# Handing out the QKV tail and the next layernorm between the heads of an attention core: a macaron block (FFN, sliding-window attention, FFN) on eight cores

## What is computed

```python
x = x + 0.5 * ffn(layernorm(x), W_r, W_k, W_v, mu_r, mu_k)
x = x + attn(layernorm(x), Wqkv, bqkv, Wo, bo, rope_cache)
x = x + 0.5 * ffn(layernorm(x), W_r, W_k, W_v, mu_r, mu_k)

def ffn(x, ...):                       # x_prev: x shifted by one row
    xr = mu_r * x + (1 - mu_r) * x_prev
    xk = mu_k * x + (1 - mu_k) * x_prev
    return sigmoid(xr @ W_r.T) * (relu(xk @ W_k.T) ** 2 @ W_v.T)

def attn(h, ...):                      # 16 heads of 64, window of 128 rows to both sides
    q, k, v = split(h @ Wqkv + bqkv)
    q, k = rope(q), rope(k)
    probs = softmax(q @ k.T / 8 + mask)
    return (probs @ v) @ Wo + bo
```

## Time and profile before

| what | before |
|---|---|
| median of 2 runs | 1699.78 us (1692.81 to 1706.74) |
| profiled execution | 1695.23 us |
| its span, slowest core | 1693.7 us |
| spans of the eight cores | 1675.3 to 1693.7 us |
| TensorE busy | 983.9 us, 58% |
| VectorE busy | 613.5 us, 36% |
| ScalarE busy | 496.7 us, 29% |

### The profile page before, as it was taken

How to read it: one execution, slowest core, us unless ns; L and a number is a source line. 1 busy time by engine, 2 the same in 40 slices (tenths; PEclk the granted TensorE clock), 3 DMA queues, 4 the chain that set the end, 5 groups by cost and what they waited for, 6 DMA issues and landing times.

```text
span 1693.7 us, 18587 instructions; the slowest of 8 cores (1675.3 to 1693.7 us)
## 1 busy us (share of the span) xinstructions
PE 983.9 (58%) x4645; PEld 416.1 (25%) x4645; DVE 613.5 (36%) x1674; ACT 496.7 (29%) x1054; POOL 38.4 (2%) x71
## 2 busy tenths in 40 slices
PE   0077614767436556636666666677666353677666
PEld 0033202223112222212222222233222121233222
DVE  1164404544312223341333444433233324444552
ACT  0233402233112332222332333333332123334231
POOL 1000000000100000000000000000000010000000
PEclk9998866888768667766777766776777565888878
DMA  9924593232651112693222222212222534233222
GB/s 165 180 55 105 104 119 97 75 93 69 207 141 31 32 38 63 95 113 68 63 63 63 63 63 53 42 39 50 45 50 50 150 103 114 69 106 94 68 69 69
DMA packets 224372, 141.15 MB, mean 83 GB/s; under 512 B 195472, under 2 KB 197648, under 8 KB 224080
## 3 DMA queue, kind: packets, MB, share of 16 engines
q0 software_dynamic: 16592, 50.08, 15.2%
q1 hardware_dynamic: 193088, 48.25, 15.0%
q10 hardware_dynamic: 14592, 41.63, 7.2%
HBM read 86.47 MB, written 39.85 MB: 75 GB/s over the span
## 4 chain that ended last, share of the span: by engine, by line
PE 36%; DVE 21%; DMA 17%; issue 9%; ACT 7%; SPq 7%; ACTq 2%; DVEq 1%; POOL 0%; POOLq 0%
PE pb L601 15%; SPq L137 7%; DMA ln_fm_s<-ln_tm 6%; PE pb L401 6%; PE pb L708 5%; DMA ln2fm_s<-ln_tm 5%; PE pb L735 4%; DVE xkm_s L346 3%; PE pb L369 3%; DVE xrm_s L341 3%; DMA kfm_s<-kpre_s 3%; DVE attn_tm_s L766 2%; PE pb L606 2%; ACT qsq L207 2%; ACT probsT_s L717 2%
## 5 line engine op out<-in xcount | busy, mean ns | idle before, releaser
L601 PE MATMUL pb<-warena,ln2fm_s 128*128 128x512 f16 x912 | 254.8, 430 | 299.3 <-DMA ln2fm_s<-ln_tm 299.3
L401 PE MATMUL pb<-warena,kfm_s 128*128 128x512 f16 x560 | 158.1, 446 | 163.7 <-DMA kfm_s<-kpre_s 163.7
L722 DVE TENSOR_TENSOR probsT_s<-probsT_s,gates_sb 128x256 bf16<-128x256 bf16 x272 | 79.4, 292 | 460.4 <-ACT probsT_s L717 421.3
L369 PE MATMUL pb<-warena,xrm_s 128*128 128x512 f16 x560 | 140.1, 408 | 127.7 <-DVE stats L211 53.1
L601 PEld LDWEIGHTS pb<-warena,ln2fm_s 128*128 128x128 f16 x912 | 87.8, 106 | 433.5 <-issue 370.7
L717 ACT ACTIVATE probsT_s<-pb 128x384 bf16<-128x384 f32 x272 | 131.7, 491 | 70.1 <-PE pb L708 61.7
L708 PE MATMUL pb<-qpl_s,kpl_s 65*128 65x128 f16 x816 | 115.9, 274 | 52.5 <-DMA kpl_s<-kaug_s 32.5
L369 PE MATMUL pb<-warena,xkm_s 128*128 128x512 f16 x560 | 126.6, 379 | 0.0
L401 PEld LDWEIGHTS pb<-warena,kfm_s 128*128 128x128 f16 x560 | 61.1, 111 | 257.9 <-issue 213.9
L379 ACT ACTIVATE r_sb_s<-pb 128x512 f16<-128x512 f32 x70 | 38.9, 595 | 274.2 <-DVE xr_sb L414 138.0
L204 ACT ACTIVATE ln_tm<-xr_sb 128x1024 f16<-128x1024 f32 x56 | 58.9, 1052 | 187.2 <-issue 63.6
(11 more groups left out here) (82 smaller groups left out, 808.9 us busy)
## 6 DMA issues: line engine op xcount, KB each, us to landing
xr_sb<-xscr POOLq DMA_DIRECT2D x36, 512.0 KB, 4.1
xr_sb<-x ACTq DMA_DIRECT2D x20, 512.0 KB, 4.6
xscr<-xr_sb ACTq DMA_DIRECT2D x19, 512.0 KB, 2.9
xscr<-xr_sb POOLq DMA_DIRECT2D x17, 512.0 KB, 3.4
out<-xr_sb ACTq DMA_DIRECT2D x16, 512.0 KB, 2.7
wqkv<-wqkv POOLq DMA_DIRECT2D x1, 6144.0 KB, 59.3
warena<-wqkv ACTq DMA_DIRECT2D x3, 2048.0 KB, 28.8
warena<-ffn ACTq DMA_DIRECT2D x3, 2048.0 KB, 20.6
```

What stands on the lines that cost most here:

```text
L369: t.matmul(pb[bk][:, :], xm[:, gp, c, 128 * ti:128 * (ti + 1)], warena[:, c, woff + 512 * js:woff + 512 * (js + 1)], start=(c == 0), stop= ...
L401: P.op("t", lambda t, bk=bk, c=c, pp=pp, js=js: t.matmul(pb[bk][:, :], kfm[:, pp, c, :], warena[:, c, 2 * DM + 512 * js:2 * DM + 512 * (js ...
L601: P.op("t", lambda t, bk=bk, c=c, par=par, js=js: t.matmul(pb[bk][:, :], ln2fm[:, par, c, :], warena[:, c, 512 * js:512 * (js + 1)], start ...
L722: P.op("v", lambda v, hp=hp, gi=gi: v.tensor_tensor(AP(probsT, hp * 384, [[4 * 384, 128], [256, 2], [1, 128]]), AP(probsT, hp * 384, [[4 * ...
```

## The change

`emit_qkv_tail` becomes a generator: it has a `yield` at eight places and stops there. A second generator, `emit_ln2_steps(j)`, holds the same instructions as `emit_ln2(j)` with five `yield`s between its pieces, the last piece being the transpose. The loop makes one feeder of the two, tail of j and then layernorm of j+1, and `emit_attn_core` takes the next piece from it at the end of each of its 18 steps. What is left is emitted behind the core; iterations without a core run the feeder in one go. No instruction is added, removed or resized. The diff, with the repeated body of the layernorm cut:

```diff
--- before.py
+++ after.py
@@ -645,6 +645,7 @@
                     .rearrange("p (h d) -> p h d", h=NH), ALU.mult),
                     waits=[("s", evw)] + ([("v", v_cq)] if which == "q" else []),
                     fence=(which == "k"), incs=[("v", 1)])
+                yield
                 P.op("v", lambda v, sv=sv, par2=par2, SS=SS: v.tensor_tensor(
                     t2[:, :].rearrange("p (h b d) -> p h b d", h=NH, b=2), sv,
                     SS[:, par2, :].rearrange("p (h b d) -> p h b d", h=NH, b=2), ALU.mult),
@@ -687,9 +693,48 @@
                  waits=[("v", rope_tok["k"])] + kpl_free[j % 4], incs=[(sn, 16)])
             tr_tok[j] = (sn, P.n(sn))
 
-        def emit_attn_core(i):
+        def emit_ln2_steps(j):
+            par = j % 2
+            sl = lambda c: stats[:, par, c:c + 1]
+            P.op("a", lambda a: a.activation(ln_tm[:, par, :], xr_sb[:, j % 8, :], AF.Copy,
+                                             accum_out=sl(0)),
+                 waits=[xtok[j]] + lnT_free[par] + stats_free.pop(par, []),
+                 incs=[("s", 1)])
+            P.op("a", lambda a: a.activation(qsq[:, :], xr_sb[:, j % 8, :], AF.Square,
+                                             accum_out=sl(1)),
+                 waits=list(qsq_free[0]) + qsq_waw[:], incs=[("s", 1)])
+            qsq_waw[:] = [("s", P.n("s"))]
+            s_sq = P.n("s")
+            yield
...
+            wtok = P.n("v")
+            yield
+            stok = emit_rstd([par], wtok)
+            yield
+            lt = emit_ln_apply(xr_sb[:, j % 8, :], par, par, stok)
+            ln2_tok[j] = lt
+            yield
+            sn = f"yl{par}"
+            P.op("y", YT(ln2fm[:, par, :, :], ln_tm[:, par, :]),
+                 waits=[("v", lt)] + ln2fm_free[par] +
+                       ([(sn, P.n(sn))] if P.n(sn) > 0 else []),
+                 incs=[(sn, 16)])
+            lnT_free[par] = [(sn, P.n(sn))]
+            y_ln2[j] = (sn, P.n(sn))
+
+        def emit_attn_core(i, feeder=None):
             par = i % 2
             win = [(i - 1) % 4, i % 4, (i + 1) % 4]
+            feed = (lambda: next(feeder, None)) if feeder is not None else (lambda: None)
             gi = 1 if i == 3 else (2 if i == 18 else 0)
             LAG = 2
             for hh in range(NH + LAG):
@@ -751,6 +796,7 @@
                             attn_un[:, h * 65:(h + 1) * 65], pb[bk][:, 0:65]),
                             waits=[("t", pv_tok[(i, h)])] + wv, incs=[("v", 1)])
                         bank_free[bk_pv] = [("v", P.n("v"))]
+                feed()
             t_last = pv_tok[(i, NH - 1)]
             for sl in win:
                 kpl_free[sl] = [("t", sc_tok[(i, NH - 1)])]
@@ -818,11 +864,16 @@
         emit_ln2(1)
         for j in range(1, NT):
             emit_qkv(j)
+
+            def mk_feeder(j=j):
+                yield from emit_qkv_tail(j)
+                if j + 1 < NT:
+                    yield from emit_ln2_steps(j + 1)
+            fd = mk_feeder()
             if QT0 <= j - 2 <= QT1:
-                emit_attn_core(j - 2)
-            emit_qkv_tail(j)
-            if j + 1 < NT:
-                emit_ln2(j + 1)
+                emit_attn_core(j - 2, feeder=fd)
+            for _ in fd:
+                pass
             if j == 1 or j == 19:
                 slot_free[j % 8] = ("v", ln2_tok[j])
             if QT0 <= j - 3 <= QT1:
```

More of the change, by code:

```diff
@@ L688, in emit_qkv_tail @@
             tr_tok[j] = (sn, P.n(sn))
-        def emit_attn_core(i):
+        def emit_ln2_steps(j):
[11 more added lines that the diff above has]
+            yield
+            P.op("v", lambda v: v.tensor_scalar(sl(2), sl(0), 1.0 / DM, None, ALU.mult),
+                 waits=[("s", s_sq)], incs=[("v", 1)])
+            P.op("v", lambda v: v.tensor_tensor(sl(3), sl(2), sl(2), ALU.mult), fence=True,
+                 incs=[("v", 1)])
+            yield
+            P.op("v", lambda v: v.scalar_tensor_tensor(sl(4), sl(1), 1.0 / DM, sl(3),
+                                                       ALU.mult, ALU.subtract),
+                 fence=True, incs=[("v", 1)])
+            P.op("v", lambda v: v.tensor_scalar(sl(4), sl(4), 1e-5, None, ALU.add),
+                 fence=True, incs=[("v", 1)])
+            wtok = P.n("v")
[4 more added lines that the diff above has]
+            ln2_tok[j] = lt
+            yield
+            sn = f"yl{par}"
[6 more added lines that the diff above has]
+        def emit_attn_core(i, feeder=None):
             par = i % 2
             win = [(i - 1) % 4, i % 4, (i + 1) % 4]
+            feed = (lambda: next(feeder, None)) if feeder is not None else (lambda: None)
             gi = 1 if i == 3 else (2 if i == 18 else 0)
```

## The result

The changed kernel takes 1539.47 us (median of 11 runs, 1531.97 to 1568.57) against 1701.37 us of the kernel before (10 runs): ratio 0.9061, 95% interval 0.9027 to 0.9094. Ratios here compare fast runs alone: in some runs of any of these kernels the cores of one die show a lower granted clock and the time is some per cent longer, as in the run of 1568.57. The forecast was 1565 in a range of 1505 to 1630, so direction and range held, and the gain was undersized by some 26 us. The profiled execution's slowest core has a span of 1538.5 us (before: 1693.7).

The account below looks back on a forecast made before the run. TensorE's 299.3 us wait for the layernorm's transpose, queued behind the core, was taken as the bound. Savings of 111+3+20 = 134 us off 1695.2 gave 1561, plus 4.6 for the timed runs: 1565, range 1505 to 1630.

Parts of the forecast that it names:

- the sum: Whole kernel: 111 us from 14 regular iterations, 3 from iteration 7, 20 from the stage's end, 134 us saved.
- the two timed runs: Kernel before: median 1699.8 us, 4.6 above the profiled execution, so the forecast went from 1561 to 1565.
- TensorE waits for `ln2fm` because of the queues, and the wait goes: Ahead of QKV: 299.3 us idle for layernorm's transpose, queued behind a core it doesn't need; regular iterations no longer wait.
- The core by hand, 20.0 us: Attention core, followed instruction by instruction with the fed steps: grows from 12.65 to 20.0 us, +7.35.
- The walk: Attention core's hand-followed timeline: Square from 5.2, reduce and max end at 9.4, layernorm's square 13.6, last PV about 20.0.
- Wo 6.3 and QKV 12.9: Behind the core: output projection stays 6.3 us; QKV falls from 15.0 to 12.9 at 2.4 GHz; period 39.2.
- The transpose comes in time, with some 4 us to spare: Behind the core: layernorm's transpose issued at 18.35, there by 22.1 to 22.5, while wo lasts until 26.3.
- Iteration 7 at 70: Iteration beside the weight casts: 70 us instead of 72.7, 3 us saved, as transposes starting earlier still mostly wait.
- The stage's end, 20 us: End of attention stage: 32.5 us wait goes, wo(17) waits for its transpose behind weight loads; 76.5 becomes 56.1 us.
- a period of 58: Iteration 7: the figure if transposes advance beside the casts from their earlier start; the sum would be 12 us lower.
- The ScalarE floor: Rival for the core: delays hide behind one another, core 16.3 us, period 35.5, total 1511; chance 0.17.
- The collapse of the lag: Rival for the core: two-head lag fails, each head 2.1 us, core 34, period 53.2, total about 1785; chance 0.03.

Follow-up runs that it names:

- the two runs with one part fed: Changed kernel with only the QKV tail fed into the core: 1578.04 us, ratio 0.931; with only the layernorm fed: 1711.64 us, ratio 1.0072.
- split step: Changed kernel with one more `yield`, between the layernorm's copy and its square: 1536.85 us, ratio 0.907.
- early rope: Changed kernel with the first four fed steps (rope of q and k) emitted ahead of the core: 1530.3 us, ratio 0.8993.
- ScalarE lighter: Changed kernel with the layernorm's copy and square reading 64 of 1024 columns, so another output: 1519.54 us, ratio 0.8957.

## Why the prediction held, point by point

The mechanism held but for the wait at the stage's end, and the sizes erred mostly to one side. In the attention stage 164 us were saved where the sum had 134: 20 of the difference are the 14 regular iterations, 11 the stage's end, and iteration 7 takes back 1. Outside the stage 9 us were lost that the forecast put at nothing (the start and the second FFN stage), so the total came out nearer to the forecast than the stage did. That part is luck. The last 4.6 us of the gap are those that the forecast added for the two timed runs: after the change the profiled execution, 1540.04 us, is no faster than the median.

- *TensorE waits for `ln2fm` because of the queues, and the wait goes.* Right. It is gone from the regular iterations, and the two runs with one part fed show that both chains had to move. I had named only the layernorm's transpose as what gates QKV; that the copies into `qaug` wait for k's transpose was not in the prediction, and it decides as soon as the tail is late.
- *The core by hand, 20.0 us.* It is 18.8 to 19.1. The growth was mis-sized by 1.2 us of 7.35. The walk had reduce and max ending at 9.4 and the layernorm's square at 13.6; the timeline, from the core's start at 875.56, has 8.6 and 12.4 (12.5 with the read of the sum):

```profile
875.56 0.51 PE L753 MATMUL pb<-qpl_s,kpl_s 65*128 65x128 f16 x6
...
882.66 1.21 DVE L666 TENSOR_REDUCE qm_s<-qsq 128x16 f32<-128x1024 f16 x1
...
884.53 0.22 ACT L674 ACTIVATE qm_s<-qm_s 128x16 f32<-128x16 f32 x1 [1.23 <-DVE probsT_s L767]
...
886.88 1.06 ACT L703 ACTIVATE qsq<-xr_sb 128x1024 f16<-128x1024 f32 x1
```

  The reduce is over at 883.9, 8.3 us into the core, and the max at 8.6. The Ln waits 1.23 us in ScalarE's queue for VectorE, as the walk said (the view names the gate that stands right behind the max); the walk was too slow already on the way there, by 0.3 us at the start of the Square (4.9 for 5.2) and by 0.8 at the max. The prediction also had both engines full. ScalarE was to be busy 14.0 us and VectorE 13.6; the row above has 12.58 and 11.53 in 18.78 us. The sums had added single durations, and operations in a row overlap in the trace: two exps take 0.87 us where twice 0.491 would be 0.98. So the core grew by waits between the engines, not because one of them was full.
- *Wo 6.3 and QKV 12.9.* QKV was exact, with a clock of 1.00 as named. Wo is 5.7 to 6.1 in most iterations, 0.2 to 0.6 less. Together with the core that makes 9.3 us saved instead of 7.9 in each of 14 iterations, 131 us for 111. This is the largest miss of the sum.
- *The transpose comes in time, with some 4 us to spare.* Right: issued at 892.56, 17.0 us into the core, and QKV(6) and all later ones don't wait for it, QKV(8) apart.
- *Iteration 7 at 70.* It was 70.7. q's transpose was issued 22 us behind the casts instead of 41, and that gained almost nothing. Before, q's alone had been slow to issue (23.48 us, k's 3.64); now both were, 21.36 and 21.54. q's landed 43.4 us after its issue, at 742.5, behind the last cast, which landed at 739.5:

```profile
699.04 21.36 SPq L137 DMA_TRANSPOSE qpl_s<-qaug_s  x1
720.55 21.54 SPq L137 DMA_TRANSPOSE kpl_s<-kaug_s  x1
742.28 1.23 SPq L137 DMA_TRANSPOSE ln2fm_s<-ln_tm  x1
```

- *The stage's end, 20 us.* This is the step where the mechanism failed, and not only a size; it is 11 us off. 2.5 of these are QKV(19), which is faster like the others and was in no term of the sum. The 32.5 us wait went as said. But wo(17) was to wait for its transpose until the weight loads were over, at T+29. The timeline shows the loads issued from 1192.28 on and the transpose of core 17 at 1196.82 (its row there takes in core 18's as well, issued at 1215.98, so 20.39 is not the time of one), and wo(17) begins at 1212.34, T+19.5, right behind core 18:

```profile
1192.28 5.81 ACTq L136 DMA_DIRECT2D warena<-ffn  x3
...
1196.82 20.39 SPq L137 DMA_TRANSPOSE attnfm_s<-attn_tm_s  x2
...
warena<-ffn ACTq DMA_DIRECT2D x1, 2048.0 KB, 24.0
attnfm_s<-attn_tm_s SPq DMA_TRANSPOSE x1, 15.2
...
PE pb L834 <- DMA attnfm_s<-attn_tm_s: 1.6, 2, 1.3
```

  The two lines with times to landing are of the last load, issued at 1193.38, and of core 17's transpose. The transpose landed at 1212.0 and the load at 1217.4. So a transpose beside loads was slowed, to 15.2 us, and went through, where I took it as blocked until their end. The last line, of the waits between 1190 and 1260 us, has 1.6 us in all. The rule of the Trainium skill that I had set aside ("DMA: Bandwidth & Descriptors", "Queues, rings and completion order", on arbitration: a DMA engine takes its queues in turn, packet by packet) fits this; beside the casts of iteration 7 the trace doesn't agree with what I drew from it, a period of 58.
- *The rivals.* The ScalarE floor (16.3 us) was not reached; ScalarE mattered more than VectorE all the same, since its fed work is paid almost one for one. The collapse of the lag did not occur. A slower outcome was near at hand in another place than I looked for it: with the same compute order and the transposes left behind the core, the kernel is 4% slower than before.
- *What would show it.* Three signs missed. The wait on `ln2fm` was to fall below 90 us and fell to 109.6. That bound didn't fit the forecast's own terms: the waits ahead of QKV(1) to QKV(4), 74.7 us after the change, were to stay, and so was some 30 us ahead of QKV(8) with iteration 7 at 70; it is 33.2. The period was to be 39 to 40 and is 37.5 to 38 in most iterations. And no wait of 10 us came ahead of wo(17).

## What to carry to other kernels

When an engine waits for work that merely stands behind other work in the queues, find every chain that ends at it (here the layernorm and the freeing of `qaug`), and move the DMA issues together with the compute, since a transpose left in its old place took back more than the whole gain. Look next for idle time of the engine that does the moved work: VectorE had the time for rope under QKV, and emitting tail and layernorm in one piece ahead of the core cost only 16 us of the 162 that the careful interleaving gained. A large background transfer in the middle of a latency-bound loop is worth cutting into pieces and spreading over the iterations: that gave another 2.5% here, and 1.1% in the kernel before.

## What was not expected of the hardware

Shorter cores did not shorten the period. With cores of 18.8, 18.5 and 17.7 us (changed kernel, split step, early rope) the late iterations all take 37.5 us, because wo takes 5.8, 6.2 and 6.95: its mean granted clock is 0.74 in the first and 0.60 in the last. In all three the core ends at 1.2 GHz (0.50), and wo is back at 2.4 GHz some 3 us after its start behind the core of 18.8 us and some 5.6 us after it behind the core of 17.7. So in these kernels small gains in the core were paid back behind it. It is no rule by the core's length. With the work in one piece ahead, cores of 20.1 to 20.4 us were followed by a wo of 5.5 to 5.9 and of 6.5 to 6.8 in turn, and with ScalarE lighter, cores of 17.2 to 17.5 by a wo of 5.4 to 6.9, with periods of 35.7 to 37.0 in turn. Why the clock returns when it does was not tested; the runs show only that it is not tied to the start of wo.
